# Both normalizations' (x - mean) * rstd moved from VectorE to GpSimd

## The reference

```
layernorm(x) = (x - mean) / sqrt(var + 1e-5)
x = x + attn(layernorm(x))     # 16 heads of 16, key j is masked for j - i > 16
x = x + ffn(layernorm(x))      # down(silu(gate(h)) * up(h)), 256 -> 1024 -> 256
```

## Time and profile before

| | us |
|---|---|
| Median of 3 runs | 620.48 |
| Lowest, highest | 620.26, 625.29 |
| The profiled execution's own time | 623.74 |
| Its span from first to last instruction | 622.0 |

### The profile page before, as it was taken

One profiled execution on the slowest core, in us unless ns is written; L12 is line 12 of the kernel. 1 busy time (PEld: TensorE's weight loads), 2 busy tenths in 40 slices (PEclk: granted clock), 3 DMA queues, 4 the chain that ended last, 5 costly groups with the idle time before them and its releaser, 6 DMA issues.

```text
span 622.0 us, 13663 instructions
## 1 busy us (share of the span) xinstructions
PE 597.9 (96%) x5376; PEld 507.2 (82%) x5376; DVE 511.4 (82%) x1031; ACT 244.2 (39%) x368; POOL 200.6 (32%) x244
## 2 busy tenths in 40 slices
PE   0899999999999999999999999999999999999997
PEld 0566545889989898888989898989888898988897
DVE  6588557898898899999999999999999999795552
ACT  1222323542443444444443444434444444344431
POOL 0531232342333242323333332324242342333322
PEclk9978756999999999999999999999999999999999
DMA  8233220322211303122221304040222212110100
GB/s 225 62 120 102 69 70 2 105 69 69 86 53 53 96 25 101 56 69 86 69 86 55 101 28 128 2 137 19 91 65 69 86 53 85 53 35 3 36 18 17
DMA packets 44111, 42.83 MB, mean 69 GB/s; under 512 B 4528, under 2 KB 42512, under 8 KB 44048
## 3 DMA queue, kind: packets, MB, share of 16 engines
q1 hardware_dynamic: 44048, 41.96, 21.8%
HBM read 12.32 MB, written 4.19 MB: 27 GB/s over the span
## 4 chain that ended last, share of the span: by engine, by line
PE 94%; DVE 4%; issue 1%; ACT 0%; POOL 0%; DVEq 0%; ACTq 0%; POOLq 0%
PE ring L625 15%; PE ring L626 12%; PE ring L627 12%; PE pair L672 9%; PE ring L704 9%; PE ring L632 9%; PE ring L633 7%; PE ring L634 7%; PE pair L696 5%; PE ring L649 4%; PE ring L616 3%; PE pair L681 2%; PE ring L687 1%; DVE M L560 1%; DVE QM L503 1%
## 5 line engine op out<-in xcount | busy, mean ns | idle before, releaser
L466 ACT ACTIVATE P<-pair 128x800 f32<-128x800 f32 x128 | 106.5, 836 | 143.4 <-PE pair L696 143.1
L625 PE MATMUL ring<-YT,WGUh 128*128 128x256 f32 x512 | 150.5, 294 | 0.1
L626 PE MATMUL ring<-YT,WGUh 128*128 128x256 f32 x512 | 144.3, 282 | 0.0
L627 PE MATMUL ring<-YT,WGUl 128*128 128x256 f32 x512 | 144.1, 281 | 0.0
L560 DVE TENSOR_REDUCE M<-pair 128x2 f32<-128x288 f32 (+1 forms) x256 | 134.6, 570 | 8.4 <-PE pair L681 4.8
L424 POOL TENSOR_TENSOR IN<-GU,IN 128x512 fp32r<-128x512 f32 x64 | 82.3, 1286 | 137.6 <-ACT IN L429 137.6
L625 PEld LDWEIGHTS ring<-YT,WGUh 128*128 128x128 f32 x512 | 96.2, 188 | 7.2 <-issue 3.2
L627 PEld LDWEIGHTS ring<-YT,WGUl 128*128 128x128 f32 x512 | 96.5, 188 | 0.0
L626 PEld LDWEIGHTS ring<-YT,WGUh 128*128 128x128 f32 x512 | 96.4, 188 | 0.0
L416 POOL TENSOR_SCALAR_AFFINE_SELECT P<-P 128x448 f32<-128x448 f32 x64 | 37.6, 587 | 181.3 <-ACT P L466 181.3
L632 PE MATMUL ring<-WD,IN 128*128 128x256 f32 x256 | 75.7, 296 | 0.1
(11 more groups left out here) (78 smaller groups left out, 1078.6 us busy)
## 6 DMA issues: line engine op xcount, KB each, us to landing
QM<-QK SPq DMA_DIRECT2D x96, 128.0 KB, 2.1
KS<-QK SPq DMA_DIRECT2D x96, 128.0 KB, 2.1
X<-x SPq DMA_DIRECT2D x32, 256.0 KB, 3.0
out<-X SPq DMA_DIRECT2D x16, 256.0 KB, 2.2
OVER<-over SPq DMA_DIRECT2D x4, 256.0 KB, 8.5
TAP<-points SPq DMA_DIRECT2D x4, 192.0 KB, 7.3
POWER<-powers SPq DMA_DIRECT2D x4, 192.0 KB, 7.6
P<-wqk SPq DMA_DIRECT2D x1, 512.0 KB, 5.4
```

The source lines that it names most:

```text
L466: nc.scalar.activation(P[:, g % 2, 2 * (n % 2):2 * (n % 2) + 2, :], pair(what, t, n)[:, :, 0:SW], ACT.Exp, scale=SCALE).then_inc(exp_done, 1)
L625: mm(o, wh[:, kb, c], act[:, 0, kb, :], start=j == 0 and kb == 0, stop=False, skip_group_check=True)
L626: mm(o, wh[:, kb, c], act[:, 1, kb, :], start=False, stop=False, skip_group_check=True)
L627: i = mm(o, wl[:, kb, c], act[:, 0, kb, :], start=False, stop=False, skip_group_check=True)
```

## The change

GpSimd takes over both calls of steps lb and mb. It waits for its own power operation (rstd_done) and signals norm_done as VectorE did. VectorE gets one new wait: before it overwrites MV in la or ma of turn t it waits until the normalization of turn t-1 has read it. The step list is the same, and no other engine's code is touched.

```
@@ gpsimd
                     nc.gpsimd.tensor_tensor(RSTD[i][:], VE[i][:], HALF[:], ALU.pow).then_inc(rstd_done[i], 1)
+                elif what in ("lb", "mb"):
+                    i, src, dst = (0, X[t % 2], X[t % 2]) if what == "lb" else (1, X1[t % N_X1], Z[t % 2])
+                    pool.wait_ge(rstd_done[i], nth({"lb": "la", "mb": "ma"}[what], t, 0))
+                    for j in range(TT):
+                        last = nc.gpsimd.tensor_scalar(dst[:, j, :], src[:, j, :], MV[i][:, j, 0:1], RSTD[i][:, j:j + 1],
+                                                       ALU.subtract, ALU.mult)
+                    last.then_inc(norm_done[i], 1)
@@ vector
                     dve.wait_ge(stats_done[i], nth(what, t, 0))
+                    if t:
+                        dve.wait_ge(norm_done[i], nth({"la": "lb", "ma": "mb"}[what], t - 1, 0))
                     for j in range(TT):
                         last = nc.vector.bn_aggr(MV[i][:, j, :], ST[i][:, j, :])
...
-                elif what in ("lb", "mb"):
-                    i, src, dst = (0, X[t % 2], X[t % 2]) if what == "lb" else (1, X1[t % N_X1], Z[t % 2])
-                    dve.wait_ge(rstd_done[i], nth({"lb": "la", "mb": "ma"}[what], t, 0))
-                    for j in range(TT):
-                        last = ts(dst[:, j, :], src[:, j, :], MV[i][:, j, 0:1], RSTD[i][:, j:j + 1], ALU.subtract, ALU.mult)
-                    last.then_inc(norm_done[i], 1)
```

## The result

The changed kernel takes 634.05 us (median of 4 runs, 631.82 to 636.85) where the kernel before takes 620.37 (4 runs beside them): ratio 1.0176, interval 1.0135 to 1.0217. By this ratio it is slower by some 11 us (8.4 to 13.5); the two medians lie 13.7 us apart. Forecast were +1.4 us and "within 1%". The profiled execution took 636.85 us and its span is 635.0 us, 13.0 more than before.

The account below looks back on a forecast made before the run. TensorE was taken as the bound, busy 597.9 of 622.0 us. The terms 0.26 + 0.95 + 0.55 + 0.03 - 0.4 = +1.4 us on the median of 620.48 gave 621.9 us, range 618.5 to 627.0 us.

Parts of the forecast that it names:

- T = 0.50 us, from the select: Assumed time T of one new GpSimd normalization call, taken from the select, nearest in inputs and elements.
- the upper bound taken from the two-input subtraction (0.75 us): Upper bound for one new GpSimd call: 2.08 ns an element and 0.22 us fixed, 0.75 us for 256 elements.
- worse end: One GpSimd call with both operations at the two-input rate one after the other: 1.3 us.
- the prediction's own formula: Added time once all five places count: 10T - 3.36 - 0.4 us, T being the time of one GpSimd call.
- the prediction's list of places: First norm of turns 0 and 1, second of turns 0, 3 and 15: +0.26, +0.95, nothing, +0.55, +0.03 us.
- Splits and selects behind the new calls: nothing: GpSimd's splits and selects behind the new calls start up to two calls later; costed at nothing.
- VectorE's relief at turn 1, -0.4 us: A removed VectorE pair stands ahead of a maximum that TensorE awaits for 0.40 us at 129.94 us: -0.4 us.
- Free up to T = 1.23 us: Second norm, turns 4 to 12: TensorE loads 2.59 us after the root, so calls up to 1.23 us cost nothing.
- Rival 1: A dear GpSimd call near 1.3 us: +10.6 us, or 631.1 us; chance 0.11 for calls beyond 1.0 us.
- Rival 2, the clock: Clock in the first turns (average grant 0.72) moves: 1.7 or 3.4 us either way, 618.5 to 625.3 us; chance 0.15.
- The SP queue: Loads of X of turn 2 and QK copies behind turn 1's normalization land at 48.85 against 48.97 us: just fits.

Follow-up runs that it names:

- the price lists: Two runs of the changed kernel with other forms of GpSimd's first norm in some settled turns, read only for call costs; 634.10 and 633.68 us.
- e9_tight: Against the kernel before, only seven pairs on GpSimd (first norm of turns 0, 1, 3; second of 0, 3, 13, 15): 638.41 us, ratio 1.0231.
- e11_turn1: Against the kernel before, one pair of 32 on GpSimd, the first norm of turn 1: ratio 1.0078.
- e2_mb: Against the kernel before, only the second norm on GpSimd, in all turns: 628.23 us, ratio 1.0089.
- e1_lb: Against the kernel before, only the first norm on GpSimd, in all turns: 629.09 us, ratio 1.0113.
- e5_first: Against the kernel before, only the first norm of turns 0, 1 and 3 on GpSimd: 629.39 us, ratio 1.0094.
- e8_tiles: Changed kernel with each normalization divided, tile 0 on VectorE and tile 1 on GpSimd: ratio 1.0052 to the kernel before.
- e3_roomy: Changed kernel with seven pairs back on VectorE (first norm of turns 0, 1, 3; second of 0, 3, 13, 15): 622.17 us, ratio 0.9995.
- e6_half: Changed kernel with GpSimd normalizing only columns 0 to 127 of each tile: 629.38 us, ratio 1.011 to the kernel before.
- e7_order: Changed kernel with GpSimd doing turn 1's first norm before the spline split and turn 3's second before the IN split: 629.03 us, ratio 1.0113.
- e10_price2: Changed kernel with five other call forms in GpSimd's first norm of turns 5 to 9, read only for call costs: 633.68 us.

## Why the prediction was wrong

- **The step that failed is "T = 0.50 us, from the select".** The term measured 1.22 us. The select was nearest in inputs and elements, but it is another kind of call, and the price lists show that here the kind counts and not the number of inputs. Even the upper bound taken from the two-input subtraction (0.75 us) was no bound: one tensor_scalar operation costs 0.92 us, more than a two-input call. Only the "worse end", two operations at that rate one after the other, 1.3 us, lay near; it had 0.11 of the chance for want of a row. Its nearness is luck: the first operation costs 2.48 ns an element and the second 0.87, not 2.08 each. With T = 1.22 the prediction's own formula gives 620.48 + 8.4 = 628.9 us, past the range; the rest is what it missed of the waits and the clock.
- **The formula held in the sum, with errors that partly cancel.** 10T - 3.76 gives +8.4 us at T = 1.22 where TensorE's idle time grew by 9.7. Place by place, forecast by the formulas and found: start 1.70 and 1.78 us; turn 1 2.39 and 2.69 (1.69 in e9_tight and 2.07 in e11_turn1, where the clock was low ahead of it; the 2.39 was read from a trace in which it was low too); Z of turn 3 1.99 and 1.69; turn 15 1.47 and 1.35; turn 0's second norm 1.29 and none, since the wait for X just ahead of it had used it up (alone, in e2_mb, it was 1.03). Missed were turn 3's first norm, 1.39 us and 0.51 for the select behind it, and turn 13, 0.43. The first stands nowhere in the prediction's list of places (e1_lb and e5_first have 0.7 to 0.8 us for it), and turn 13 was said to have as much room as the settled turns. GpSimd's pair also starts 0.11 us behind the root and not 0.04 (11.77 + 0.72 to 12.60 us at the start).
- **"Splits and selects behind the new calls: nothing"** was wrong by the 0.51 us above, and by 0.4 us for a split of IN in the last turn of e1_lb, e2_mb and e8_tiles.
- **VectorE's relief at turn 1, -0.4 us**: in the trace the wait at 129.94 us has gone, as it has in e3_roomy; in e1_lb, with that pair back on VectorE, it stands again (0.40 us). Another wait for M is 0.25 us longer in the changed kernel, so their total is still 2.2 us. VectorE's busy time fell by 25.1 us and not by 32: 64 quiet calls of 0.41 us are 26, and the rest of the groups' means was waiting, as the prediction says.
- **"Free up to T = 1.23 us" in the settled turns** was right for the second norm alone: in e2_mb T is 1.22 and a turn still takes 33.77 us. With both norms on GpSimd it takes 33.81, which the prediction had at 33.77. With T = 1.3 us there would be waits too by the same reckoning; that was not run.
- **Rival 1** was the case that came. It assumed 1.3 us and gave 631.1. Its threshold, more than 1% from T = 1.0 us on, looks too high: e6_half with T = 0.805 us already has ratio 1.011 (1.0078 to 1.0142).
- **Rival 2, the clock**, was right in being there and wrong in being even to both sides: the mean loss was above that of the kernel before in all six kernels in which TensorE waits about 1.7 us or more for X of turn 1 (the change, e1_lb, e5_first, e6_half, e9_tight, e11_turn1: +2.2 to +7.7 us), and within 0.8 us of it in the five where this wait is absent or at most 1.5 us. But the loss also counts idle time. The means of time rise beyond the idle time of the traces by less: 0.5 us in e5_first, 1.3 in e1_lb, 1.5 in e11_turn1, 2.2 in e6_half and 6.0 in e9_tight, each with an uncertainty of about 1 us. So a cost of the clock is clear in e9_tight and e6_half; that the wait of turn 1 causes it is likely and not shown. Why e9_tight lost 7.7 stays open.
- **The SP queue** behind turn 1's normalization did not show in the changed kernel, where both sides grew alike, and did in e7_order, 0.89 us.

## What to carry to other kernels

Before work goes to GpSimd, list for each place how long after its input the first reader comes, then put the real price of that very form of call into the list: an engine that is idle on average (32% busy here) is not yet room, and the room is a property of each place, of what stands ahead of it in the engine's order and, in the first turns, of the clock. Take the price from a row of the same instruction with the same number of operations; where there is none, let the forecast's chances hang on it. And count the unsettled first and last turns separately: 7 of 32 moved pairs paid nearly the whole price, and leaving those on VectorE makes the move free, though no gain either, since TensorE is the bound.

## What the runs showed of the hardware

- On GpSimd a tensor_scalar of one operation over 128x256 fp32 takes 0.85 to 0.93 us, of two 1.07 to 1.22, while a two-input tensor_tensor takes 0.61 and a copy 0.39. Written as two two-input calls with broadcast mean and rstd over both tiles, the normalization would take about 2 x 1.04 = 2.1 us instead of 2.43; this is an estimate from the rows of e10_price2 and was not run.
- The Trainium skill, "GPSIMD Engine Reference", section "Engine selection", calls one-input elementwise work on GpSimd "roughly line-rate" and two-input work about twice as slow as VectorE. Here the copy goes 256 elements in 0.39 us, but one-input arithmetic was dearer than two-input arithmetic (0.92 against 0.61 us), and the fused pair three times VectorE's 0.41.
- TensorE's grant in this kernel moves in the first 130 us alone and is 1.00 behind them in the profiled execution of every kernel; a spread of 9 us in the time of one and the same kernel (617.0 to 626.1 us) goes with losses of 14 to 26 us there.
- A lower clock ahead of a place makes the place roomier: TensorE's wait for the same pair of turn 1 was 2.69 us where the grant was full until 43 us, and 1.69 us where it was 0.50 from 41 us on.
